# Splitting the operands of the block attention's output projection into high and low parts

## The chip, the cores and the metric

The kernel runs on one core of one Trainium2 chip. The metric is the device time of the whole program in microseconds. All times in the rows are microseconds from the start of the profiled execution's span, unless a column says ns.

## The reference

The input is `x`, 8 images of 384 channels and 32 x 32 pixels. The reference applies three layers, each added to its input: a group norm with a deformable 3 x 3 convolution, batch norm and GELU; a block attention over tokens; and an attention whose heads are chosen by a router, followed by a layer norm. Only the second matters here. With `t` the 8 x 1024 tokens of 384 channels after the first layer, cut into blocks of 128:

```python
t = t + _L1_attn_ref(_ln_t(t), w_qkv, w_ln, w_proj)
...
qkv = xb @ w_qkv                       # xb: one block of normalised tokens, 128 x 384
q, k, v = jnp.split(qkv, 3, axis=-1)
q, k = (rms(q), rms(k))                # root mean square norm over 384, times w_ln
...
q = q * cos + _rotate(q) * sin         # 12 heads of 32 channels; k in the same way
att = softmax(where(causal, q k^T / sqrt(32), -max))
y = att @ v
y = y @ w_proj                         # the output projection, 384 x 384
```

## The kernel before

The program is one launch of five stages, one after the other: `offsets_and_table`, `deform_conv`, `batch_norm_gelu`, `block_attention` and `head_attention`. In each, every engine has an instruction stream of its own, and only semaphores order them; a `wait_ge` holds back all that stands behind it on the same engine. The engines are TensorE (PE; its weight loads PEld), VectorE (DVE), ScalarE (ACT), GpSimd (POOL) and SyncE (SP).

The change lies in `block_attention` (from L902). It works on 64 blocks of 128 tokens, which stay in SBUF as `y`. The work of a block is spread over several turns, and in turn `i` different engines work on blocks `i - 1` to `i + 3`. Turn 0 is written out, turns 1 to 60 run as a hardware loop of 30 passes with two turns each (`turns`), and turns 61 to 63 are written out again. The order in each engine's `turn` is fixed by hand.

What one block goes through, with the function that does it:

- VectorE normalises the tokens into `h` (`norm`, L1066). TensorE transposes them into the bank `b_ht` (`turn_h`, L1256). ScalarE copies that, rounded to fp32r, into `h_high` (`copy_h`, L1179), and VectorE writes the remainder `b_ht - h_high` into `h_low` (`low`, L1073).
- TensorE makes Q, K and V (`make_qkv`, L1281). Each third is nine fp32r matmuls: high times high, high times low, low times high, over three chunks of 128 channels. The weights were split once ahead of the blocks: ScalarE copies `w_high` (L1240), and VectorE subtracts `w_low` (L1162).
- ScalarE sums squares of Q and K (`squares`, L1214), VectorE forms the means (`mean_square`, L1078), and GpSimd takes the power -1/2 (`rqk`, L1035). VectorE multiplies Q and K by that and by the rotation's tables (`rotate`, L1087 and L1093), and GpSimd adds the two products (L1042).
- TensorE transposes Q and K (`turn_qk`), ScalarE copies them out (`copy_qk`), and TensorE makes the 12 heads' scores and adds the causal mask by four bf16 matmuls (`scores`, L1299 and L1303).
- VectorE takes the row maxima in two halves (`maxima`, L1102 and L1108), each followed by six exponentials with their accumulator reads on ScalarE (`exponentials`, L1205). VectorE divides by the sums (`divide`, L1118 and L1121).
- TensorE transposes the probabilities (`turn_prob`, L1311), ScalarE copies them (`copy_prob`, L1184), and TensorE multiplies them with V, into `b_ht` once more (`mix`, L1324). ScalarE copies this mixed tile to `mixed_t` (`copy_mixed`, L1179).
- TensorE applies the output projection (`project`, L1332): three fp32 products over the chunks, which the trace shows as six instructions, again into `b_ht`. VectorE adds the result to `y` (`add`, L1129) and takes the tokens' statistics (`statistics`, L1137 to L1140). SyncE stores the block.

The orders around the change, in turn `i`:

- VectorE: `maxima(i)`, `norm(i+3)`, `add(i-1)`, `divide(i)` in two halves, `mean_square(i+2)`, `low(i+3)`, `rotate(i+2)`, `statistics(i-1)`. The last instruction of `statistics` is the small L1140.
- ScalarE: `copy_mixed(i-1)`, `exponentials(i)`, `squares(i+2)`, `copy_h(i+3)`, `copy_prob(i)`, `copy_qk(i+1)`, `copy_v(i+2)`.
- TensorE: `make_qkv(i+2)`, with `project(i-1)` between its first and second third, then `turn_h(i+3)`, `turn_prob(i)`, `turn_qk(i+1)`, `mix(i)`, `scores(i+1)`.

The bank `b_ht` is written in turn by `turn_h`, `mix` and `project`; `turn_h` waits for `out_done`, which `add` raises. `w_ln` holds two rows of 384 numbers that GpSimd multiplies into the tables `rot_a` and `rot_b` ahead of the blocks; it raises `tables` behind that, and VectorE and TensorE wait for `tables` first. Much SBUF is shared in time: the probabilities lie where `w_qkv` was.

Of the kernel before, what the change touches and what calls it, by code (L numbers as in the profile page):

```python
# [8 lines left out]
ACT = mybir.ActivationFunctionType  # L9
# [5 lines left out]
P = 128  # L15
BATCH, C, SIDE = 8, 384, 32
# [885 lines left out]
def block_attention(nc, io, sem, sb, bank, ident, neg_half, y, tokens, token_stats, token_rstd, block_consts, consts,  # L902
# [11 lines left out]
    with ExitStack() as mem:  # L914
        w_qkv, w_proj, rot_a, rot_b, w_ln, causal = block_consts
        ident_lo = sb(mem, "d_ident_lo", [P], BF16)
        causal_lo = sb(mem, "d_causal_lo", [CH, P], BF16)
        h = sb(mem, "d_h", [C])
        w_high = sb(mem, "d_w_high", [CH, 3 * C], F32R)
        w_low = sb(mem, "d_w_low", [CH, 3 * C], F32R)  # L920
        h_high = sb(mem, "d_h_high", [CH, P], F32R)
        h_low = sb(mem, "d_h_low", [CH, P], F32R)
        v = [sb(mem, f"d_v{u}", [C]) for u in range(2)]
        square = sb(mem, "d_square", [2, C])
        ssq = sb(mem, "d_ssq", [2])
        ms = sb(mem, "d_ms", [2])
# [10 lines left out]
                        for i in range(2))  # L937
        psum = sb(mem, "d_psum", [HEADS])
        inv = sb(mem, "d_inv", [HEADS])
        mixed_t = sb(mem, "d_mixed_t", [CH, P])  # L940
        tst = sb(mem, "d_tst", [6])
        tmv = sb(mem, "d_tmv", [1, 2])
        tvar = sb(mem, "d_tvar", [BLOCKS])
# [27 lines left out]
        pt_psum = sem("d_pt_psum")  # L971
        pt_ready = sem("d_pt_ready")
        av_psum = sem("d_av_psum")
        mt_ready = sem("d_mt_ready")
        out_psum = sem("d_out_psum")
        out_done = sem("d_out_done")
        stored = sem("d_stored")
# [16 lines left out]
        def exists(n):  # L994

            return not known(n) or 0 <= n < BLOCKS
# [13 lines left out]
        with nc.Block() as block:  # L1010
# [47 lines left out]
            def _(dve):  # L1058
# [11 lines left out]
                def low(n):  # L1070
# [2 lines left out]
                    nc.vector.tensor_tensor(h_low[:], b_ht[:, 0:C].rearrange("p (o q) -> p o q", q=P), h_high[:],  # L1073
                                            ALU.subtract).then_inc(ht_ready, 1)

                def mean_square(n):
                    dve.wait_ge(squared, n + 1)
                    nc.vector.tensor_scalar(ms[:], ssq[:], 1.0 / C, 1e-6, ALU.mult, ALU.add).then_inc(ms_ready, 1)  # L1078
# [61 lines left out]
                    nc.vector.tensor_scalar(tvar[:, blk], tmv[:, 0, 1:2], 1e-5, None, ALU.add).then_inc(token_var, 1)  # L1140

                def turn(i, u):
                    maxima(i)
                    if exists(i + 3):
                        norm(i + 3)
                    if exists(i - 1):
                        add(i - 1)
                    for half in range(2):
                        divide(i, half)
                    if exists(i + 2):  # L1150
                        mean_square(i + 2)
                    if exists(i + 3):
                        low(i + 3)
                    if exists(i + 2):
                        rotate(i + 2)
                    if exists(i - 1):
                        statistics(i - 1)
# [11 lines left out]
                low(2)  # L1169
                mean_square(1)  # L1170
                rotate(1)
                turns(turn)(dve)
                add(END)
                statistics(END)

            @block.scalar
            def _(act):
                def three(out, src):
                    return nc.scalar.activation(out, src[:, 0:C].rearrange("p (o q) -> p o q", q=P), ACT.Copy)  # L1179
# [15 lines left out]

                def copy_mixed(n):
                    act.wait_ge(av_psum, n + 1)
                    three(mixed_t[:], b_ht).then_inc(mt_ready, 1)

                def exponentials(n):  # L1200
                    for half, heads in enumerate(HALVES):
# [36 lines left out]
                act.wait_ge(consts, 16 * CONSTS)  # L1238
                for o in range(CH):
                    nc.scalar.activation(w_high[:, o], w_qkv[:, o], ACT.Copy).then_inc(w_split, 1)  # L1240
                for n in range(2):
                    copy_h(n)
                    squares(n)
                    copy_v(n, n)
# [6 lines left out]
            def _(pe):  # L1251
# [76 lines left out]

                def project(n):
                    pe.wait_ge(mt_ready, n + 1)  # L1330
                    for o in range(CH):
                        last = nc.tensor.matmul(b_ht[:, 0:C], mixed_t[:, o], w_proj[:, o], start=(o == 0),  # L1332
                                                stop=(o == CH - 1))
                    last.then_inc(out_psum, 1)

                def turn(i, u):
# [18 lines left out]
                turn_h(2)  # L1355
                turn_qk(0)
                scores(0)
                turns(turn)(pe)
                project(END)


# [1102 lines left out]
```

## Time and profile before

| | |
|---|---|
| median of 3 runs | 3693.16 us (3691.4 to 3697.67) |
| profiled execution | 3696.41 us |
| its span, first to last instruction | 3694.4 us |
| mean granted TensorE clock | 0.953 |
| TensorE busy (matmul) | 3335.8 us, 90% |
| VectorE busy | 2714.7 us, 73% |
| ScalarE busy | 2257.3 us, 61% |
| GpSimd busy | 1456.9 us, 39% |

The durations further on come from the one profiled execution. A timeline row gives the start, the duration (of all the instructions merged into the row, where x is over 1), the engine, the line, the operation, what it writes and reads with their sizes, how many instructions the row stands for, and in brackets the idle time of the engine ahead of it with the one that ended it. Successive instructions of an engine overlap in part, so the distance between two starts is less than the duration shown. Busy shares over the whole span mix stages with different limits; the block attention's loop lies between about 1705 and 2412 us.

### The profile page before, as it was taken

What the parts mean: (1) busy time and instruction counts of PE and PEld (TensorE: products, weight loads), DVE (VectorE), ACT (ScalarE), POOL (GpSimd) and SP (SyncE); (2) the same over time, 40 slices, a digit from 0 to 9 for tenths busy, and PEclk for the clock granted to TensorE, in tenths of its full rate; (3) what the DMA queues carried; (4) which work ended last, traced back from release to release, by engine and by line L of the source; (5) the groups of instructions that cost most, each with busy time, mean ns of one, the idle gap of its engine ahead of it and who ended that gap; (6) DMA issues with size and microseconds to landing.
All of it is one profiled execution on the core that took longest, in us unless ns stands there. A gap on an engine that the chain in (4) does not pass through costs nothing. (4 is left out here: it accounts for less than half of the span.)

```text
span 3694.4 us, 65555 instructions
## 1 busy us (share of the span) xinstructions
PE 3335.8 (90%) x18046; PEld 1927.0 (52%) x18046; DVE 2714.7 (73%) x5169; ACT 2257.3 (61%) x5369; POOL 1456.9 (39%) x1544
## 2 busy tenths in 40 slices
PE   7969999999999999947999999968888888888897
PEld 3434444444444444436888888844444444434443
DVE  4468888888888888756888888846677677766765
ACT  3434444444444444355777777746877778777785
POOL 2144444444444444272222222221254454544535
PEclk9979999999999999968999999978999999999997
DMA  9999989889999899541000000011222322232221
GB/s 362 370 356 345 333 333 351 324 328 338 349 340 342 336 343 347 221 171 37 17 17 17 17 17 17 17 64 45 84 74 64 91 72 65 78 87 64 59 66 55
DMA packets 230577, 647.44 MB, mean 175 GB/s; under 512 B 31142, under 2 KB 127942, under 8 KB 229958
## 3 DMA queue, kind: packets, MB, share of 16 engines
q0 software_dynamic: 82944, 453.02, 32.7%
q1 hardware_dynamic: 147398, 191.91, 16.4%
q8 instruction: 71, 1.16, 0.1%
q14 instruction: 164, 1.34, 0.1%
HBM read 520.21 MB, written 79.18 MB: 162 GB/s over the span
## 5 line engine op out<-in xcount | busy, mean ns | idle before, releaser
L697 PE MATMUL b_acc<-b_sampled,b_w 128*128 128x512 f32 x2592 | 1210.8, 594 | 0.0
L632 DVE SCALAR_TENSOR_TENSOR b_mix<-shared,b_weight,b_mix 128x384 f32<-128x384 f32 x864 | 531.8, 621 | 140.6 <-ACT b_mix L655 82.6
L697 PEld LDWEIGHTS b_acc<-b_sampled,b_w 128*128 128x128 f32 x2592 | 449.1, 191 | 347.5 <-issue 347.5
L664 ACT ACTIVATE b_sampled<-b_tps 128x384 f32<-128x384 f32 x576 | 282.7, 491 | 566.5 <-PE b_tps L715 556.6
L1988 DVE TENSOR_REDUCE e_neg_top<-e_next 128x1 f32<-128x1024 f32 x384 | 469.8, 1224 | 211.1 <-PE e_next L2301 171.4
L632 DVE SCALAR_TENSOR_TENSOR b_mix<-b_got,b_weight,b_mix 128x384 f32<-128x384 f32 x864 | 530.8, 619 | 92.6 <-ACT b_mix L655 55.9
L2140 ACT ACTIVATE e_unused<-e_next,e_neg_top 128x1024 bf16<-128x1024 f32 x384 | 430.1, 1120 | 117.1 <-DVE e_neg_top L1988 104.8
L2155 ACT ACTIVATE e_prob<-e_s 128x512 f32<-128x512 f32 x768 | 416.9, 598 | 125.3 <-PE e_s L2313 124.3
L588 POOL DMA_INDIRECT shared<-corner_table,b_index x288 | 294.7, 1023 | 418.7 <-DVE b_mix L632 291.9
L588 POOL DMA_INDIRECT b_got<-corner_table,b_index x288 | 292.6, 1016 | 356.8 <-DVE b_mix L632 282.7
L715 PEld LDWEIGHTS b_tps<-ident,b_mix 128*128 128x128 f32 x1728 | 223.0, 142 | 371.9 <-issue 328.2
L1205 ACT ACTIVATE d_w_qkv<-d_back,d_neg_top 128x128 f32<-128x128 f32 x768 | 269.6, 390 | 135.6 <-DVE d_neg_top L1108 135.6
L715 PE MATMUL b_tps<-ident,b_mix 128*128 128x128 f32 x1728 | 286.9, 275 | 57.2 <-DVE b_mix L632 50.9
L2301 PE MATMUL e_next<-e_stack 96*128 96x512 f32 x768 | 302.3, 476 | 22.6 <-issue 9.4
L2313 PE MATMUL e_s<-e_stack 98*128 98x512 f32 x768 | 271.3, 429 | 5.8 <-ACT e_prob L2155 4.8
L655 ACT ACTIVATE b_mix<-shared,b_weight 128x384 f32<-128x384 f32 x288 | 177.3, 615 | 106.5 <-ACT b_sampled L664 54.4
L2327 PE MATMUL e_acc<-e_prob,e_v 128*32 128x512 f32 x1536 | 213.4, 629 | 7.1 <-DVE e_ctx L2002 5.6
L2301 PEld LDWEIGHTS e_next<-e_stack 96*128 96x128 f32 x768 | 127.5, 198 | 159.3 <-issue 105.5
L655 ACT ACTIVATE b_mix<-b_got,b_weight 128x384 f32<-128x384 f32 x288 | 177.2, 615 | 54.5 <-ACT b_sampled L664 50.5
L1035 POOL TENSOR_TENSOR d_rqk<-d_ms,neg_half 128x2 f32<-128x2 f32 x64 | 44.9, 702 | 412.5 <-DVE d_ms L1078 412.5
L2313 PEld LDWEIGHTS e_s<-e_stack 98*128 98x128 f32 x768 | 148.8, 198 | 65.0 <-ACT e_prob L2155 34.2
L1205 ACT ACTIVATION_READ_ACCUMULATOR d_w_qkv<-d_back,d_neg_top 128x1 f32 x768 | 176.4, 230 | 0.0
(225 smaller groups left out, 5360.2 us busy)
## 6 DMA issues: line engine op xcount, KB each, us to landing
corner_table<-y SPq DMA_DIRECT2D x32, 1536.0 KB, 14.8
e_stack<-e_high SPq DMA_DIRECT2D x384, 64.0 KB, 2.0
shared<-in_x SPq DMA_DIRECT2D x8, 1536.0 KB, 10.1
c_x<-in_x SPq DMA_DIRECT2D x16, 768.0 KB, 4.4
tokens<-y SPq DMA_DIRECT2D x64, 192.0 KB, 1.9
e_tok<-tokens SPq DMA_DIRECT2D x8, 1536.0 KB, 7.3
e_stack<-e_low SPq DMA_DIRECT2D x192, 64.0 KB, 2.0
shared<-tokens SPq DMA_DIRECT2D x8, 1536.0 KB, 7.2
```

The costliest lines, as they stand in the source:

```text
L588: nc.gpsimd.indirect_dma_start(out=got[t % SLOTS][:], out_offset=None, in_=table[:, :], in_offset=bass.IndirectOffsetOnAxis(ap=index[g][:, ...
L632: ins = nc.vector.scalar_tensor_tensor(dst[:], src[:, q * C:(q + 1) * C], weight[g][:, q, k, i:i + 1], dst[:], ALU.mult, ALU.add)
L655: nc.scalar.activation(mix[t % MIXES][:], got[t % SLOTS][:, 0:C], ACT.Copy, scale=weight[g][:, 0, k, i:i + 1]).then_inc(begun, 1)
L664: nc.scalar.activation(sampled[s % 2][:, :, i * P:(i + 1) * P], tps[t % 2][:, 0:C].rearrange("p (o q) -> p o q", q=P), ACT.Copy).then_inc( ...
L697: last = nc.tensor.matmul(acc[g][co][:], w_conv[:, k, ci, co * P:(co + 1) * P], sampled[s % 2][:, ci], start=(k == 0 and ci == 0), stop=(k ...
L715: last = nc.tensor.transpose(tps[t % 2][:, o * P:(o + 1) * P], mix[t % MIXES][:, o * P:(o + 1) * P], ident[:])
L1205: last = nc.scalar.activation(prob[:, head], b_s[r][:, c * P:(c + 1) * P], ACT.Exp, bias=neg_top[:, head:head + 1], scale=SCALE, accum_out ...
L1988: nc.vector.reduce_max(neg_top[s % 2][:, t:t + 1], b_next[t % 2][:], AX.X, negate=True).then_inc(top_ready, 1)
L2140: nc.scalar.activation(unused[t % 2][:], b_next[t % 2][:], ACT.Exp, bias=neg_top[s % 2][:, t:t + 1], accum_out=den[s % 2][:, t:t + 1]).the ...
L2155: nc.scalar.activation(prob[(2 * c + f) % 8][:], b_s[f][:], ACT.Exp).then_inc(prob_ready, 1)
L2301: last = nc.tensor.matmul(b_next[t % 2][:, f * HALF:(f + 1) * HALF], stack[k][0:96, 0, t * P:(t + 1) * P], stack[k][0:96, 1, f * HALF:(f + ...
L2313: nc.tensor.matmul(b_s[f][:], stack[k][0:98, 1, c * P:(c + 1) * P], stack[k][0:98, 0, f * HALF:(f + 1) * HALF], start=True, stop=True).the ...
```

## The change

The projection's operands are split as those of `make_qkv` are. `mixed_t` goes; ScalarE writes the rounded copy `m_high`, and VectorE's new `mixed_low` writes the remainder `m_low` at the head of the turn, ahead of `maxima`. `project` waits for `m_low` and issues nine fp32r matmuls. The weights `w_proj` are split once: ScalarE's `p_high` behind the copies of `w_high`, VectorE's `p_low` behind `rotate(1)` and ahead of the turns, and TensorE waits for both ahead of the turns. To make room in SBUF, `h` and the second `v` buffer lie in the two rows of `w_ln`.

```diff
--- before.py
+++ after.py
@@ -915,12 +915,12 @@
         w_qkv, w_proj, rot_a, rot_b, w_ln, causal = block_consts
         ident_lo = sb(mem, "d_ident_lo", [P], BF16)
         causal_lo = sb(mem, "d_causal_lo", [CH, P], BF16)
-        h = sb(mem, "d_h", [C])
+        h = w_ln[:, 0]
         w_high = sb(mem, "d_w_high", [CH, 3 * C], F32R)
         w_low = sb(mem, "d_w_low", [CH, 3 * C], F32R)
         h_high = sb(mem, "d_h_high", [CH, P], F32R)
         h_low = sb(mem, "d_h_low", [CH, P], F32R)
-        v = [sb(mem, f"d_v{u}", [C]) for u in range(2)]
+        v = [sb(mem, "d_v0", [C]), w_ln[:, 1]]
         square = sb(mem, "d_square", [2, C])
         ssq = sb(mem, "d_ssq", [2])
         ms = sb(mem, "d_ms", [2])
@@ -937,7 +937,10 @@
                         for i in range(2))
         psum = sb(mem, "d_psum", [HEADS])
         inv = sb(mem, "d_inv", [HEADS])
-        mixed_t = sb(mem, "d_mixed_t", [CH, P])
+        p_high = sb(mem, "d_p_high", [CH, C], F32R)
+        p_low = sb(mem, "d_p_low", [CH, C], F32R)
+        m_high = sb(mem, "d_m_high", [CH, P], F32R)
+        m_low = sb(mem, "d_m_low", [CH, P], F32R)
         tst = sb(mem, "d_tst", [6])
         tmv = sb(mem, "d_tmv", [1, 2])
         tvar = sb(mem, "d_tvar", [BLOCKS])
@@ -971,7 +974,9 @@
         pt_psum = sem("d_pt_psum")
         pt_ready = sem("d_pt_ready")
         av_psum = sem("d_av_psum")
+        mt_high = sem("d_mt_high")
         mt_ready = sem("d_mt_ready")
+        p_split = sem("d_p_split")
         out_psum = sem("d_out_psum")
         out_done = sem("d_out_done")
         stored = sem("d_stored")
@@ -1072,6 +1077,12 @@
                     dve.wait_ge(ht_high, n + 1)
                     nc.vector.tensor_tensor(h_low[:], b_ht[:, 0:C].rearrange("p (o q) -> p o q", q=P), h_high[:],
                                             ALU.subtract).then_inc(ht_ready, 1)
+
+                def mixed_low(n):
+
+                    dve.wait_ge(mt_high, n + 1)
+                    nc.vector.tensor_tensor(m_low[:], b_ht[:, 0:C].rearrange("p (o q) -> p o q", q=P), m_high[:],
+                                            ALU.subtract).then_inc(mt_ready, 1)
 
                 def mean_square(n):
                     dve.wait_ge(squared, n + 1)
@@ -1140,6 +1151,8 @@
                     nc.vector.tensor_scalar(tvar[:, blk], tmv[:, 0, 1:2], 1e-5, None, ALU.add).then_inc(token_var, 1)
 
                 def turn(i, u):
+                    if exists(i - 1):
+                        mixed_low(i - 1)
                     maxima(i)
                     if exists(i + 3):
                         norm(i + 3)
@@ -1169,7 +1182,10 @@
                 low(2)
                 mean_square(1)
                 rotate(1)
+                dve.wait_ge(p_split, 1)
+                nc.vector.tensor_tensor(p_low[:], w_proj[:], p_high[:], ALU.subtract).then_inc(p_split, 1)
                 turns(turn)(dve)
+                mixed_low(END)
                 add(END)
                 statistics(END)
 
@@ -1195,7 +1211,7 @@
 
                 def copy_mixed(n):
                     act.wait_ge(av_psum, n + 1)
-                    three(mixed_t[:], b_ht).then_inc(mt_ready, 1)
+                    three(m_high[:], b_ht).then_inc(mt_high, 1)
 
                 def exponentials(n):
                     for half, heads in enumerate(HALVES):
@@ -1238,6 +1254,7 @@
                 act.wait_ge(consts, 16 * CONSTS)
                 for o in range(CH):
                     nc.scalar.activation(w_high[:, o], w_qkv[:, o], ACT.Copy).then_inc(w_split, 1)
+                nc.scalar.activation(p_high[:], w_proj[:], ACT.Copy).then_inc(p_split, 1)
                 for n in range(2):
                     copy_h(n)
                     squares(n)
@@ -1328,9 +1345,10 @@
 
                 def project(n):
                     pe.wait_ge(mt_ready, n + 1)
-                    for o in range(CH):
-                        last = nc.tensor.matmul(b_ht[:, 0:C], mixed_t[:, o], w_proj[:, o], start=(o == 0),
-                                                stop=(o == CH - 1))
+                    for i, (a, b) in enumerate(((m_high, p_high), (m_high, p_low), (m_low, p_high))):
+                        for o in range(CH):
+                            last = nc.tensor.matmul(b_ht[:, 0:C], a[:, o], b[:, o], start=(i == 0 and o == 0),
+                                                    stop=(i == 2 and o == CH - 1))
                     last.then_inc(out_psum, 1)
 
                 def turn(i, u):
@@ -1355,6 +1373,7 @@
                 turn_h(2)
                 turn_qk(0)
                 scores(0)
+                pe.wait_ge(p_split, 2)
                 turns(turn)(pe)
                 project(END)
```

## Rows read from the trace of the kernel before

**Rows 1.** Windows of the trace; the block loop's 60 turns; columns: engine busy us, PEclk, DMA, GB/s

```profile
1716.19:2411.22 695.03, 695.03 (x6362) 589.69 (x6361) 571.98 (x1440) 535.13 (x2160) 195.38 (x240) 1.00 0.05 17
```

**Rows 2.** Waits within the loop; columns: total us, times, longest us

```profile
ACT d_w_qkv L1205 <- DVE d_neg_top L1108: 126.3, 60, 2.2
...
DVE d_h_low L1073 <- ACT d_h_high L1179: 27.3, 60, 0.6
...
DVE d_top L1102 <- PE d_back L1303: 11.1, 30, 0.9
```

**Rows 3.** Timeline of VectorE over two turns; columns: start us, us, engine, line

```profile
1994.52 1.02 DVE L1102 TENSOR_REDUCE d_top<-d_back 128x3 f32<-128x384 f32 x2 [0.35 <-PE d_back L1303]
...
2002.30 0.62 DVE L1087 SCALAR_TENSOR_TENSOR d_part_a<-d_front,d_rqk,d_rot_a 128x384 f32<-128x384 f32 x1
...
2005.76 0.14 DVE L1140 TENSOR_SCALAR d_tvar<-d_tmv 128x1 f32 x1
...
2005.82 1.01 DVE L1102 TENSOR_REDUCE d_top<-d_back 128x3 f32<-128x384 f32 x2
...
2013.28 0.56 DVE L1073 TENSOR_TENSOR d_h_low<-d_front,d_h_high 128x384 fp32r<-128x384 f32 x1 [0.61 <-ACT d_h_high L1179]
...
2013.75 0.61 DVE L1087 SCALAR_TENSOR_TENSOR d_part_a<-d_front,d_rqk,d_rot_a 128x384 f32<-128x384 f32 x1
...
2017.20 0.14 DVE L1140 TENSOR_SCALAR d_tvar<-d_tmv 128x1 f32 x1
...
2017.69 0.56 DVE L1102 TENSOR_REDUCE d_top<-d_back 128x3 f32<-128x384 f32 x1 [0.35 <-PE d_back L1303]
```

**Rows 4.** The same two turns on ScalarE and GpSimd

```profile
1995.78 0.37 ACT L1205 ACTIVATE d_w_qkv<-d_back,d_neg_top 128x128 f32<-128x128 f32 x1 [2.24 <-DVE d_neg_top L1108]
...
1999.82 0.27 ACT L1205 ACTIVATION_READ_ACCUMULATOR d_w_qkv<-d_back,d_neg_top 128x1 f32 x1
...
2001.46 0.70 POOL L1035 TENSOR_TENSOR d_rqk<-d_ms,neg_half 128x2 f32<-128x2 f32 x1 [6.54 <-DVE d_ms L1078]
...
2004.60 0.49 ACT L1179 ACTIVATE d_mixed_t<-d_front 128x384 f32<-128x384 f32 x1
...
2011.10 0.26 ACT L1205 ACTIVATION_READ_ACCUMULATOR d_w_qkv<-d_back,d_neg_top 128x1 f32 x1
```

**Rows 5.** Last score matmuls on TensorE, and the maxima of turn 1

```profile
1715.33 0.82 PE L1303 MATMUL d_back<-d_causal_lo,d_ident_lo 128*128 128x384 bf16 x4
...
1716.19 1.02 DVE L1102 TENSOR_REDUCE d_top<-d_back 128x3 f32<-128x384 f32 x2 [0.86 <-PE d_back L1303]
...
2004.90 0.82 PE L1303 MATMUL d_back<-d_causal_lo,d_ident_lo 128*128 128x384 bf16 x4
...
2016.49 0.82 PE L1303 MATMUL d_back<-d_causal_lo,d_ident_lo 128*128 128x384 bf16 x4
```

**Rows 6.** Timeline of TensorE's weight loads (PEld) around one output projection

```profile
1994.86 0.53 PEld L1281 LDWEIGHTS d_front<-d_w_high,d_h_low 128*128 128x128 f32 x3
...
1995.38 1.65 PEld L1332 LDWEIGHTS d_front<-d_w_proj,d_mixed_t 128*128 128x128 f32 x6
...
1997.17 0.69 PEld L1281 LDWEIGHTS d_front<-d_w_high,d_h_high 128*128 128x128 f32 x3
...
1997.83 0.55 PEld L1281 LDWEIGHTS d_front<-d_w_low,d_h_high 128*128 128x128 f32 x3
```

**Rows 7.** One group by line (busy, mean ns), then timeline of prologue and tail

```profile
L1073 DVE TENSOR_TENSOR d_h_low<-d_front,d_h_high 128x384 fp32r<-128x384 f32 x60 | 33.5, 558 | 27.3 <-ACT d_h_high L1179 27.3
...
1673.50 3.27 ACT L1240 ACTIVATE d_w_high<-d_w_qkv 128x1152 fp32r<-128x1152 f32 x3 [5.92 <-PEq L774]
...
1676.84 3.89 DVE L1162 TENSOR_TENSOR d_w_low<-d_w_qkv,d_w_high 128x1152 fp32r<-128x1152 f32 x3
...
1682.13 0.97 PEld L1281 LDWEIGHTS d_front<-d_w_low,d_h_high 128*128 128x128 f32 x3
...
2445.93 3.97 PE L1332 MATMUL d_front<-d_w_proj,d_mixed_t 128*128 128x384 f32 x6 [0.61 <-ACT d_mixed_t L1179]
```

## The prediction

> **What bounds the kernel now.** I read the windows of the trace first, then the waits inside the block loop, then the timeline of single turns engine by engine. The change touches only the block attention. From the row maxima of turn 1 to those of turn 61, 60 turns, the trace spans 695.03 us, so a turn takes 11.58 us. There TensorE shows as busy all the time at granted clock 1.00, which is the 2.4 GHz level, while VectorE is busy 572 us, 9.5 us of each turn [rows 1]. Read alone, that says that TensorE is the bound and that any VectorE work fits into 2 us of idle time. The waits say to look closer. ScalarE waits for VectorE's `d_neg_top` in each of the 60 turns, 126.3 us together, over 2 us each. VectorE waits for the high half of h in 60 turns (27.3 us) and for the scores in only 30 [rows 2].
>
> So I followed VectorE and ScalarE once round, over two turns, since the loop holds two turns per pass [rows 3, 4]. Maxima start at 1994.52. ScalarE begins its exponentials 1.26 us later and issues the last accumulator read at 1999.82. Then come VectorE's second `divide`, `mean_square`, GpSimd's power (2001.46 to 2002.16) and the rotation at 2002.30, which is 2.48 us after that last read and 0.14 us after the power ends. The rotation and the statistics follow without a stall up to the last small instruction at 2005.76, and the next maxima start at 2005.82. The legs of this turn are 7.78, 3.46 and 0.06 us. The next turn's are 7.93, 3.45 and 0.49: rotation at 2013.75, last small instruction at 2017.20, maxima at 2017.69. The sum is 23.17 us, twice the 11.58 us turn. The ring is therefore nearly closed by VectorE, ScalarE and GpSimd alone. The only slack that I find is in the second turn: the rotation starts 2.65 us after the last read at 2011.10, where 2.48 would do, because the high half of h comes late from TensorE. That is 0.17 us in two turns.
>
> The trace names the scores as what ended the idle 0.35 us ahead of the maxima at 2017.69. I don't believe it. In turn 1, where VectorE had nothing else to do, the maxima began 0.86 us after the last score matmuls started (1715.33 to 1716.19); by that the scores of the pair were there at 2005.76 and 2017.35 [rows 5]. The maxima at 2017.69 were thus 0.34 us later than TensorE required. The late ones come every second turn, at the loop's edge, so I read the gap as VectorE's sequencer going round the loop.
>
> **The change, part by part.**
>
> *TensorE's projection* (`project`) loses six plain fp32 instructions and gets nine fp32r ones. Going by weight loads, the six occupy 1995.38 to 1997.17, 1.79 us, and the group behind takes 0.66 instead of 0.52 us, 0.14 more: 1.93 us. Three of the new form take 0.52 us (1994.86 to 1995.38), so nine take 1.56 us [rows 6]. TensorE saves 0.37 us a turn.
>
> *The subtraction `mixed_low`* is added on VectorE at the head of every turn, ahead of `maxima`. The nearest row is `low`: same tiles, shapes and types, 558 ns [rows 7]. Behind `low` the next instruction starts after 0.47 us (2013.28 to 2013.75) [rows 3], and that is what a queued instruction costs on the ring. It stands between the last small instruction and the maxima, exactly where VectorE has no cover in either turn. Bounds: from below, part of it hides in the loop's edge (first rival); from above, the full 0.56 us [rows 7] plus the 0.06 that the step from the last small instruction to the maxima takes [rows 3], 0.62. I take 0.47, since a wait already satisfied and registers worked out ahead cost nothing between `low` and the rotation. Its wait for `mt_high` queues `maxima`, hence ScalarE's exponentials, behind it. The wait should be empty: the copy of the mixed tile ends at 2005.09, 0.67 us ahead of the last small instruction [rows 3, 4], and TensorE, on which it depends, will be early rather than late.
>
> *The ring's new length.* 23.17 less the slack 0.17 plus 2 x 0.47 is 23.94 us in two turns, 0.77 more, or 11.97 a turn. TensorE would need only 11.58 - 0.37 = 11.21, so its saving turns into a wait of some 0.8 us ahead of `turn_prob`, where it must wait for the normalised probabilities. Thirty pairs cost +23.1 us. TensorE's term then has no weight: were the nine matmuls free, or as long as the six, the ring would stay.
>
> *`project` now waits for `m_low`* instead of the copied tile. Behind that wait stand the K and V parts of the next QKV product. TensorE reaches `project` 0.86 us after the maxima start (1994.52 and 1995.38) [rows 3, 6]; `m_low` will end 0.56 us after the point where they start now. If TensorE comes up to 0.5 us sooner, it waits at most some 0.2 us, and of its 0.8 us of new slack that costs nothing.
>
> *Splitting the projection's weights.* ScalarE's extra copy is 1,152 wide, like each of the three that take 3.27 us from 1673.50. It ends near 1677.9 and is hidden by VectorE's three subtractions, 3.89 us from 1676.84 [rows 7]. VectorE's own extra one, 3.89 / 3 = 1.3 us, stands right ahead of turn 0's maxima, which today start with no idle behind the rotation: +1.3. If `copy_h` of block 0 slipped instead, it would have until the third subtraction is done.
>
> *Edges.* Turn 1's subtraction fits in VectorE's 0.86 us of idle [rows 5]. Turn 62's costs about 0.4. In turn 63 VectorE waits long for TensorE, and it is hidden. The last block's projection is bare: six instructions take 3.97 us at the lower clock level; nine take 9 x 0.32 = 2.9 (three take 0.97 in the prologue at that level) plus some 0.2 of tail, and 0.6 goes to the subtraction [rows 7]: -0.3. Together -0.3 + 0.4 + 1.3 = +1.4.
>
> *The rest* costs nothing: h and the second v lie in `w_ln`, which GpSimd has read before `tables` lets anyone write there; the copy on ScalarE only changes its output type.
>
> **Sum:** +23.1 + 1.4 = +24.5 us. The profiled execution took 3696.4 us (span 3694.4), which gives 3721; it lies 3.3 above the median of the runs, and against the median 3693.2 the forecast is 3717.7 us, 0.7% slower.
>
> **A rule against the trace.** The gap at the loop's edge is 0.49 us where the other turn has 0.06 [rows 3], and by turn 1's 0.86 us the scores did not cause it. The Trainium skill, page "Advanced Engine Details and Errata", section "Control Flow Timing", gives a compare-and-branch about 108 ns. By that, 0.3 us of the gap would be something else, and a queued instruction could run inside it. The rows' reading stands in my sum; the rule's outcome is the first rival.
>
> **Rivals.**
> *1. The edge hides part of the subtraction.* If only about 0.1 of the 0.43 us that the edge adds is the sequencer's, 0.3 us of one subtraction in two is covered: 0.77 - 0.3 = 0.47 a pair, 14 us in thirty, 3709 with the edges. For it: the trace itself names TensorE there. Against: the 0.86 us of turn 1. Chance 0.16.
> *2. TensorE is the bound, and the kernel gets faster.* This is the plain reading of [rows 1]: 695 of 695 us busy, VectorE idle 2 us a turn. The subtraction then fits, and a turn shrinks by 0.37: 60 x 0.37 = 22 us less, plus 1.3 for the weights' split, 3672 us. It decides if the ring with the subtraction in it is shorter than 11.21 us, that is, if it has 0.77 us of slack a turn that I didn't see. Against it stands that its legs add up to the measured turn. Chance 0.10.
> *3. Gain and loss cancel.* The subtraction's 0.47 is mostly covered and TensorE's 0.37 reaches the end only in part, so the time stays within some microseconds of 3693. It needs two covers at once. Chance 0.05.
> *4. A dearer subtraction* (0.62 a turn, or a late `mt_high`): 1.07 a pair, 32 us, 3727. It lies inside the forecast's own range. Chance 0.12. That TensorE's new waits drop its clock has 0.02; the loop has no row to price it by.
> The forecast itself has 0.55.
>
> **How the numbers follow.** The time is the forecast's, 3718. The range runs from 3704, which takes in the first rival, to 3728, the dearer subtraction; outside stay the faster case, the cancelling one and the clock, 0.17. A measurement of this kernel can tell about 0.2%, 7 us, from no change. Faster has 0.10, same 0.06 (the cancelling case and the low edge of rival 1), slower 0.84.
>
> **What would show it.** Right: 60 turns take about 718 us; VectorE goes from the last small instruction through `mixed_low` to the maxima with under 0.1 us of stall in the even turns; the high half of h no longer waits for TensorE; a new wait of TensorE for the `divide` product appears, 0.5 to 1 us a turn; nine projection matmuls take 1.56 us. Wrong: turns under 11.5 us, or the maxima still ended by the scores. If the loop's edge shows less than 0.4 us between the last small instruction and `mixed_low`, rival 1 holds.

## The result and the profile after

The changed kernel takes 3719.49 us, the median of 4 runs (3718.12 to 3722.48); the kernel before, on the same chips, 3694.94 us, the median of 4 (3691.40 to 3697.67). The ratio is 1.0071, with a 95% interval of 1.0058 to 1.0083. The forecast was 3718.

The first view again is the windows of the trace, here from the maxima of turn 1 to those of turn 61. Columns as in [rows 1].

```profile
1711.47:2425.72 714.25, 682.05 (x6546) 613.88 (x6545) 597.23 (x1501) 527.19 (x2160) 195.46 (x241) 1.00 0.05 17
```

The 60 turns take 714.25 us where they took 695.03. TensorE, which showed as busy in all of the time, is now idle for 32 us of it, and the granted clock is still 1.00. The waits within this stretch, of VectorE, ScalarE and TensorE's weight loads, answer to [rows 2]:

```profile
ACT d_w_qkv L1221 <- DVE d_neg_top L1119: 169.6, 60, 3.0
...
DVE d_inv L1129 <- ACT d_w_qkv L1221: 50.9, 75, 0.9
...
DVE d_part_a L1098 <- POOL d_rqk L1040: 14.4, 59, 0.3
...
DVE d_m_low L1084 <- issue: 10.1, 29, 0.4
...
DVE d_h_low L1078 <- ACT d_h_high L1195: 0.3, 1, 0.3
...
PEld d_back L1328 <- DVE d_w_qkv L1132: 46.2, 59, 1.0
```

ScalarE's wait for `d_neg_top` has grown from 126.3 to 169.6 us. VectorE waits for the high half of h once instead of 60 times; it waits for GpSimd's power (`d_rqk`) and, mostly ahead of the second divide, for the exponentials. TensorE has a new wait in 59 of 60 turns, 46.2 us in all, 0.77 us a turn: it stands in front of `turn_prob` until VectorE has divided. Two turns of VectorE answer to [rows 3]:

```profile
1996.84 0.56 DVE L1084 TENSOR_TENSOR d_m_low<-d_front,d_m_high 128x384 fp32r<-128x384 f32 x1 [0.35 <-issue]
...
1997.32 1.01 DVE L1113 TENSOR_REDUCE d_top<-d_back 128x3 f32<-128x384 f32 x2
...
2002.89 0.19 DVE L1129 RECIPROCAL d_inv<-d_psum 128x6 f32<-128x6 f32 x1 [0.77 <-ACT d_w_qkv L1221]
...
2005.07 0.62 DVE L1098 SCALAR_TENSOR_TENSOR d_part_a<-d_front,d_rqk,d_rot_a 128x384 f32<-128x384 f32 x1 [0.30 <-POOL d_rqk L1040]
...
2008.53 0.14 DVE L1151 TENSOR_SCALAR d_tvar<-d_tmv 128x1 f32 x1
...
2008.60 0.54 DVE L1084 TENSOR_TENSOR d_m_low<-d_front,d_m_high 128x384 fp32r<-128x384 f32 x1
...
2009.06 1.01 DVE L1113 TENSOR_REDUCE d_top<-d_back 128x3 f32<-128x384 f32 x2
...
2016.71 0.62 DVE L1098 SCALAR_TENSOR_TENSOR d_part_a<-d_front,d_rqk,d_rot_a 128x384 f32<-128x384 f32 x1 [0.20 <-POOL d_rqk L1040]
...
2020.17 0.14 DVE L1151 TENSOR_SCALAR d_tvar<-d_tmv 128x1 f32 x1
...
2020.66 0.56 DVE L1084 TENSOR_TENSOR d_m_low<-d_front,d_m_high 128x384 fp32r<-128x384 f32 x1 [0.35 <-issue]
...
2021.13 1.01 DVE L1113 TENSOR_REDUCE d_top<-d_back 128x3 f32<-128x384 f32 x2
```

And on ScalarE and GpSimd, in the second of them (answering to [rows 4]):

```profile
2014.34 0.26 ACT L1221 ACTIVATION_READ_ACCUMULATOR d_w_qkv<-d_back,d_neg_top 128x1 f32 x1
...
2015.97 0.70 POOL L1040 TENSOR_TENSOR d_rqk<-d_ms,neg_half 128x2 f32<-128x2 f32 x1 [6.55 <-DVE d_ms L1089]
```

Each turn now has the subtraction L1084 between the last small instruction and the maxima. It costs 2009.06 - 2008.60 = 0.46 us in the one turn. At the loop's edge the gap of 0.49 us is there as before, with the subtraction and its 0.47 us behind it (2020.17, 2020.66, 2021.13). The pair, from 1997.32 to 2021.13, takes 23.81 us where it took 23.17. Note that the profile calls the gap at the edge "issue" now; ahead of it stand no scores that it could name. TensorE's weight loads answer to [rows 6]:

```profile
2009.48 0.54 PEld L1350 LDWEIGHTS d_front<-d_p_high,d_m_high 128*128 128x128 f32 x3
...
2010.01 0.54 PEld L1350 LDWEIGHTS d_front<-d_p_low,d_m_high 128*128 128x128 f32 x3
...
2010.53 0.54 PEld L1350 LDWEIGHTS d_front<-d_p_high,d_m_low 128*128 128x128 f32 x3
...
2011.05 0.54 PEld L1298 LDWEIGHTS d_front<-d_w_high,d_h_high 128*128 128x128 f32 x3
...
2015.87 0.20 PEld L1328 LDWEIGHTS d_back<-ident,d_w_qkv 128*128 128x128 f32 x2 [0.62 <-DVE d_w_qkv L1132]
```

The nine projection matmuls take from 2009.48 to 2011.05, 1.57 us, and the group behind them is not stretched. So TensorE did save its 0.37 us, and more than gave it back 5 us later in the wait at 2015.87.

To say where the rest of the time went, I cut every profile at five points: the first normalisation of block 0, the maxima of turn 1, the maxima of turn 61, the last block's add, and the end. The table has all the profiles of this study, one execution each, in us; the runs named there come in the next section.

```
                   ahead of    to maxima   60 turns   to the     behind
                   block 0     of turn 1              last add   it
before             1676.45     39.74       695.03     38.73      1244.45
same_before        1676.39     40.15       695.04     38.82      1244.50
padded_code        1679.13     39.43       694.54     38.97      1245.13
two_semaphores     1673.19     38.92       694.54     40.03      1241.72
after              1669.98     41.49       714.25     38.79      1253.99
same_after         1676.18     41.14       714.38     38.78      1253.82
after_padded       1675.95     41.62       714.43     39.42      1248.28
no_subtraction     1679.92     40.87       687.26     37.79      1249.06
two_subtractions   1676.77     41.95       743.05     40.97      1256.16
fp32_projection    1675.64     40.69       714.60     41.10      1251.57
four_turns         1676.16     41.06       706.76     39.13      1242.29
moved              1674.43     40.88       686.47     36.33      1247.09
moved_four         1673.82     40.56       680.83     36.21      1243.28
moved_fp32         1674.75     41.24       706.93     36.60      1248.98
```

The loop's column repeats itself to 0.2 us in the same kernel, and to 0.5 us in the two that differ from the kernel before only by idle instructions or unused semaphores. That makes it the measure for every question about the turns. The stages around the block attention do not repeat so well: 24.1 us more span in the changed kernel's first profile are +1.75, +19.22 and +0.06 in the block attention, together +21.0, and -6.5 ahead of it and +9.5 behind it. The second profiles of the two kernels differ by 29.4 us: +1.0, +19.3 and 0.0 in the block attention, together +20.3, and -0.2 ahead of it and +9.3 behind it.

### The profile page after: what moved, and what is told of

Read it like the earlier page. It is cut to its first block and busy times, and to the rows that moved or that the text cites. A ratio compares the mean times of both kernels' runs of the same rounds, so it can differ in the third digit from the quotient of the medians.

```text
span 3718.5 us, 66035 instructions
## 1 busy us (share of the span) xinstructions
PE 3329.7 (90%) x18238; PEld 1955.1 (53%) x18238; DVE 2741.6 (74%) x5234; ACT 2248.8 (60%) x5370; POOL 1454.5 (39%) x1544
## 5 line engine op out<-in xcount | busy, mean ns | idle before, releaser
L2346 PE MATMUL e_acc<-e_prob,e_v 128*32 128x512 f32 x1536 | 222.0, 652 | 7.1 <-DVE e_ctx L2021 5.5
```

The lines of the kernel that those rows point to most:

```text
L2346: last = nc.tensor.matmul(b_acc[at:at + HD], v[u][:, c, s], prob[(2 * c + f) % 8][:], start=(pair == 0), stop=(pair == PAIRS - 1))
```

## The experiments

The theory under test: a turn's length is a ring over VectorE, ScalarE and GpSimd, and what stands at the head of VectorE's turn is paid in full, while TensorE has slack. The main rival: TensorE is the bound, as its busy share says. Each experiment starts from the changed kernel, except where its text names another one. `moved` changes three places at once. The cuts in the code are marked by dots.

**The subtraction taken out (no_subtraction).**

```diff
                 def project(n):
-                    pe.wait_ge(mt_ready, n + 1)
-                    for i, (a, b) in enumerate(((m_high, p_high), (m_high, p_low), (m_low, p_high))):
+                    pe.wait_ge(mt_high, n + 1)
+                    for i, (a, b) in enumerate(((m_high, p_high), (m_high, p_low), (m_high, p_high))):
...
                 def turn(i, u):
-                    if exists(i - 1):
-                        mixed_low(i - 1)
                     maxima(i)
```

> The changed kernel without VectorE's subtraction: project waits for ScalarE's rounded copy and multiplies it a second time with p_high in the place of m_low, so the low part of the mixed tile is left out of the result. Still nine matmuls, and the weights are still split. Theory (a ring of VectorE, ScalarE and GpSimd sets the turn, TensorE has slack): the loop's pair of turns goes to the ring without the subtraction, 23.17 - 0.27 = 22.9 us, 11.45 a turn, 687 us for 60 turns, and the time to about 3694.9 - 8 + 1.3 = 3688 us. Rival (TensorE was the bound before): a turn takes 11.21 us, 673 us for 60 turns, time about 3674 us.

Measured: 60 turns in 687.26 us, pairs of 22.91; 3693.95 us in all, ratio 1.0001 (0.9992 to 1.0010). The loop says theory, within 0.3 us; TensorE's bound would have been 673. VectorE's and TensorE's waits in the loop, and one of its edges on TensorE and VectorE:

```profile
DVE d_top L1113 <- issue: 10.1, 29, 0.4
...
PEld d_back L1325 <- DVE d_w_qkv L1132: 19.8, 58, 0.5
...
2017.28 0.82 PE L1317 MATMUL d_back<-d_causal_lo,d_ident_lo 128*128 128x384 bf16 x4
...
2018.29 0.14 DVE L1151 TENSOR_SCALAR d_tvar<-d_tmv 128x1 f32 x1
...
2018.78 1.02 DVE L1113 TENSOR_REDUCE d_top<-d_back 128x3 f32<-128x384 f32 x2 [0.35 <-issue]
```

With nothing of the change left on VectorE's turns and TensorE relieved of 0.37 us a turn, the loop is only 7.8 us shorter than before, 0.13 us a turn, and TensorE waits 19.8 us for the divides. This is the most that the faster projection could bring in the old order. It also says what bound the kernel before: TensorE, which had no idle time there [rows 1], was the longer of two chains, but by only 0.13 us a turn, and past that the ring takes over. The wait rows also bear on how I read the gap ahead of the maxima. Here the last score matmuls start 1.50 us ahead of the maxima (2017.28 to 2018.78), against 1.20 before [rows 5, 3], and the gap of 0.49 us (2018.29 to 2018.78) is still there, in 29 waits of 0.35 us with no releaser. In the profile of before the same gap was put down to the scores [rows 2]. The whole time came out 6 us above what I expected; the loop did not, so that lies in the other stages of the table.

**The subtraction made twice (two_subtractions).**

```diff
                     dve.wait_ge(mt_high, n + 1)
+                    nc.vector.tensor_tensor(spare[:], b_ht[:, 0:C].rearrange("p (o q) -> p o q", q=P), m_high[:],
+                                            ALU.subtract)
                     nc.vector.tensor_tensor(m_low[:], b_ht[:, 0:C].rearrange("p (o q) -> p o q", q=P), m_high[:],
                                             ALU.subtract).then_inc(mt_ready, 1)
```

> The changed kernel with the same subtraction made twice, the first result into a part of w_proj that nobody reads any more. Theory: every microsecond at the head of VectorE's turn is paid in full, so 60 turns cost 60 x 0.47 = 28 us more than the changed kernel's 714 in the loop: 742 us, and 3748 us in all. Rival (part of what stands there hides in the loop's edge): 0.3 us less in each of 30 pairs, 3739 us. Rival (VectorE has idle time for it): no change, 3719 us.

Measured: 60 turns in 743.05 us, 28.8 us or 0.48 a turn more than the changed kernel; 3754.90 us in all, ratio 1.0155 (1.0140 to 1.0171). VectorE at the head of a turn:

```profile
2002.56 0.14 DVE L1154 TENSOR_SCALAR d_tvar<-d_tmv 128x1 f32 x1
...
2002.62 0.54 DVE L1085 TENSOR_TENSOR d_w_proj<-d_front,d_m_high 128x384 f32<-128x384 f32 x1
...
2003.09 0.54 DVE L1087 TENSOR_TENSOR d_m_low<-d_front,d_m_high 128x384 fp32r<-128x384 f32 x1
...
2003.55 1.01 DVE L1116 TENSOR_REDUCE d_top<-d_back 128x3 f32<-128x384 f32 x2
```

The rows step by 0.47 and 0.46 us. With no, one and two subtractions the loop takes 687.3, 714.3 and 743.1: 0.45 us for the first and 0.48 for the second. The first is hardly cheaper than the second, so there is no slack left in which it could have hidden. Both rivals, one with idle time and one with a cover at the edge, fall. The whole time is 7 us above the expected 3748, the loop only 1.

**The old projection behind the new wait (fp32_projection).**

```diff
-        m_high = sb(mem, "d_m_high", [CH, P], F32R)
+        m_high = sb(mem, "d_m_high", [CH, P])
...
-                    for i, (a, b) in enumerate(((m_high, p_high), (m_high, p_low), (m_low, p_high))):
-                        for o in range(CH):
-                            last = nc.tensor.matmul(b_ht[:, 0:C], a[:, o], b[:, o], start=(i == 0 and o == 0),
-                                                    stop=(i == 2 and o == CH - 1))
+                    for o in range(CH):
+                        last = nc.tensor.matmul(b_ht[:, 0:C], m_high[:, o], w_proj[:, o], start=(o == 0),
+                                                stop=(o == CH - 1))
```

> The changed kernel with the old projection behind the new wait: ScalarE copies the mixed tile unrounded, VectorE still subtracts and TensorE still waits for that, but then it issues the six plain fp32 instructions on the unrounded copy and w_proj. Theory: TensorE's 0.37 us more a turn find slack, the loop stays at 714 us and the time at 3719 us within 2 us. Rival (TensorE's saving counts in the changed kernel): 60 x 0.37 = 22 us more, 3741 us.

Measured: 60 turns in 714.60 us, against 714.25 to 714.43 in three profiles of the changed kernel's order; 3721.28 us in all, 2 above the expected 3719, ratio 1.0076 (1.0062 to 1.0090). The wait of TensorE for the divides:

```profile
PEld d_back L1328 <- DVE d_w_qkv L1132: 23.5, 58, 0.6
```

This row is the neatest of the study. TensorE works 0.37 us longer in each turn, and its wait falls from 46.2 to 23.5 us, by 22.7 us, 0.38 a turn. The loop doesn't move (at most 0.4 us in 714). In the changed kernel the nine matmuls bring nothing.

**The subtraction off the ring (moved).**

```diff
                 def turn(i, u):
-                    if exists(i - 1):
-                        mixed_low(i - 1)
                     maxima(i)
+                    if exists(i - 1):
+                        mixed_low(i - 1)
                     if exists(i + 3):
                         norm(i + 3)
+                    divide(i, 0)
                     if exists(i - 1):
                         add(i - 1)
-                    for half in range(2):
-                        divide(i, half)
+                    divide(i, 1)
...
-                        if w == 1 and between is not None:
+                        if w == 2 and between is not None:
                             project(between)
```

> The changed kernel with the subtraction taken off the ring: VectorE makes it behind maxima instead of ahead, TensorE's project stands between the second and the last third of the QKV product instead of between the first two, and VectorE's add stands between the two divides. There VectorE waits for ScalarE's exponentials anyway, 0.77 us in the changed kernel. Theory: the ring has the length that it has without the subtraction, 22.92 us a pair as measured, TensorE needs 11.21 a turn, so the loop goes from 714 to about 688 us and the time to 3694 us or a little under. Rival (the add, now late, or the projection holds the second divide): a turn stays above 11.6 us, the loop above 696 us, 3701 us or more.

Measured: 60 turns in 686.47 us; 3689.10 us in all, ratio 0.9990 (0.9981 to 0.9999) to the kernel before. The same instructions as in the changed kernel, in another order, give 27.8 us back in the loop. The loop was expected at about 688 us and the whole time at 3694 or a little under. VectorE in one turn:

```profile
2012.95 1.02 DVE L1113 TENSOR_REDUCE d_top<-d_back 128x3 f32<-128x384 f32 x2 [0.35 <-PE d_back L1320]
...
2015.21 0.55 DVE L1084 TENSOR_TENSOR d_m_low<-d_front,d_m_high 128x384 fp32r<-128x384 f32 x1
...
2016.67 0.96 DVE L1132 TENSOR_TENSOR d_w_qkv<-d_w_qkv,d_inv 128x768 f32<-128x768 f32 x1
...
2017.79 0.55 DVE L1140 TENSOR_TENSOR y<-y,d_front 128x384 f32 x1 [0.16 <-PE d_front L1350]
...
2018.54 0.19 DVE L1129 RECIPROCAL d_inv<-d_psum 128x6 f32<-128x6 f32 x1 [0.19 <-ACT d_w_qkv L1221]
```

The subtraction at 2015.21 runs while ScalarE makes the exponentials, and the second divide's reciprocal at 2018.54 comes 5.59 us behind the maxima. In the changed kernel's turn behind an edge it came 5.57 us behind them (1997.32 to 2002.89). Nothing that the ring needs has moved. How much of the gain belongs to each of the three moves, and what the moved order alone would do to the kernel before, no run here shows; but the loop is as short as with no subtraction at all (687.26 us), so the subtraction costs nothing in its new place.

**Four turns in a pass (four_turns, moved_four).**

```diff
-                with eng.Fori(0, (BLOCKS - 4) // 2) as j:
-                    turn(2 * j + 1, 1)
-                    turn(2 * j + 2, 0)
+                with eng.Fori(0, (BLOCKS - 4) // 4) as j:
+                    for k in range(1, 5):
+                        turn(4 * j + k, k % 2)
```

> The changed kernel with four turns in a pass of the loop on every engine instead of two: 15 passes. Theory (the edge costs VectorE's sequencer 0.42 us on the ring): 15 edges less give 15 x 0.42 = 6.3 us, the loop goes from 714.3 to 708 us, 3713 us in all. Rival (only about 0.1 us of the gap is the edge's): 1.6 us less. Rival (the longer loop body no longer fits where instructions are kept and each pass waits for them): a gap of more than 0.5 us at each edge, and the loop no shorter than 714 us.

Measured on the changed kernel: 60 turns in 706.76 us, 7.5 us less for 15 edges, 0.50 us an edge where 0.42 was expected; 3704.88 us in all, 8 below the expected 3713, ratio 1.0031 (1.0021 to 1.0041). The gap at VectorE's edge is there half as often as in the waits of the changed kernel (29 times, 10.1 us):

```profile
DVE d_m_low L1084 <- issue: 4.8, 14, 0.4
```

On average over the turns the gap alone is worth 0.41 us. The other 0.1 us is in the turn that follows an edge. There the rotation starts 2.47 us behind the last accumulator read, and 2.38 us behind it in the three others of a pass. In the changed kernel every second turn has the 2.47, here only every fourth.

> The moved kernel (subtraction behind maxima, projection one third later, add between the divides) with four turns in a pass of the loop. Theory: 15 edges less on the ring, each worth 0.31 us (a turn with an edge took 11.60 in the moved kernel, one without 11.29) to 0.5 us (714.3 - 706.8 in 15, measured on the changed kernel): the loop goes from 686.5 to 679 to 682 us, the time to about 3684 us. Rival (TensorE's chain through the wait for m_low, 11.22 us a turn, takes over at once): loop not under 684 us.

Measured with the moved subtraction: 60 turns in 680.83 us; 3683.08 us in all, ratio 0.9970 (0.9958 to 0.9982). This version, which leaves nothing of the computation out and has the split projection, takes 0.3% less than the kernel before and is the fastest of the study. Part of that is the fewer edges, 5.6 us for 15 of them (0.38 each in this order), which the kernel before might gain as well; that wasn't run. A turn is at 11.35 us, close to the 11.2 that TensorE needs. The whole time came within a microsecond of what was expected, the loop inside its bounds.

**The old projection in the moved order (moved_fp32).** The edit is that of fp32_projection, on the moved kernel.

> The moved kernel with the six plain fp32 instructions in the projection, on an unrounded copy and w_proj; the subtraction and the wait for it stay. Here TensorE has only 0.2 us of slack a turn: from maxima to the projection 2.86 us, from there to the next maxima 8.36 us, 11.22 together. Theory: 0.37 us more make this chain 11.59 us, longer than the ring's 11.44, so the loop goes from 686.5 to 695 to 700 us, about 3699 us in all. That would show that the nine matmuls are worth their gain only once the subtraction is off the ring. Rival (TensorE still has slack): loop 686 to 688 us.

Measured: 60 turns in 706.93 us, 20.5 more than the moved kernel, 0.34 a turn; 3712.08 us in all, ratio 1.0042 (1.0027 to 1.0058). The direction is the theory's, the size is not: I expected 9 to 14 us. The whole time is 13 us above the expected 3699. The wait of VectorE's add says why:

```profile
DVE y L1140 <- PE d_front L1349: 31.1, 58, 0.5
...
2010.59 1.01 DVE L1113 TENSOR_REDUCE d_top<-d_back 128x3 f32<-128x384 f32 x2
...
2015.80 0.56 DVE L1140 TENSOR_TENSOR y<-y,d_front 128x384 f32 x1 [0.54 <-PE d_front L1349]
2016.50 0.19 DVE L1129 RECIPROCAL d_inv<-d_psum 128x6 f32<-128x6 f32 x1
```

It waits in 58 turns, 0.54 us each (0.18 in the moved kernel), and behind it stands the second divide, which in this order comes after the add. The divide's reciprocal now starts 5.91 us behind the maxima (2010.59 to 2016.50), where it was 5.59, and waits for no exponential. So a longer projection goes straight into the ring by way of the add, and not only into TensorE's own chain of 11.59 us that I had worked out: a turn takes 11.78. In the moved order TensorE's 0.37 us count nearly in full; in the changed kernel's they count nothing.

**What drifts, and what the stage behind it does (same_before, same_after, padded_code, two_semaphores, after_padded).** The first two are the two kernels, run again. The others add only instructions that do nothing, or semaphores. The edit of padded_code, on the kernel before:

```diff
                 add(END)
                 statistics(END)
+                for _ in range(8):
+                    dve.nop(nofuse=True)
...
                 copy_mixed(END)
+                act.nop(nofuse=True)
...
                 project(END)
+                for _ in range(12):
+                    pe.nop(nofuse=True)
```

That of two_semaphores, on the kernel before:

```diff
+        unused = [sem(f"d_unused{i}") for i in range(2)]
         mt_ready = sem("d_mt_ready")
```

That of after_padded, on the changed kernel, on VectorE and in the same way on TensorE:

```diff
+                for _ in range(32):
+                    dve.nop(nofuse=True)
                 dve.wait_ge(tables, 3 + CH)
```

> The kernel before once more, for how far the other stages drift from one execution to the next. The changed kernel's profile has 6.5 us less ahead of the first block and 9.5 us more behind the last add than the profile of before. If that is drift, this profile shows differences of several microseconds in the same places, with the loop at 695 us again. If it is the change's doing (other addresses of the code or of the tiles), both stages come out within 1 us of the first profile: first normalisation at 1676, 1244 us behind the last add.

> The kernel before with instructions that do nothing behind the last turn of the block attention: 12 on TensorE, 8 on VectorE, 1 on ScalarE, about as many as the change adds to each engine's program ahead of the last stage. All four changed kernels have 4.6 to 11.7 us more behind the last add than the two profiles of before (1244.5 us). If the place of the last stage's code is the cause, this one has more than 1248 us there; if not, 1245 to 1246 us. The block loop stays at 695.0 us either way.

> The kernel before with two more semaphores that nobody uses, as many as the change adds, so that those of the last stage get the numbers that they have in the changed kernel. If the numbers matter, there are over 1248 us behind the last add; if not, 1244.5 us as before. The block loop stays at 695.0 us.

> The changed kernel once more. Its first profile had 1254.0 us behind the last add, where four profiles of before and its padded copies have 1241.7 to 1245.1. If that belongs to the changed kernel, it has over 1250 us again; if it drifts from execution to execution, it can come out at 1247 us or less. The block loop stays at 714.3 us, and the first normalisation lies between 1670 and 1680 us.

> The changed kernel with 32 instructions that do nothing at the head of the block attention on TensorE and on VectorE, where both wait some 4 us or more for the tables anyway. Both profiles of the changed kernel show 1253.8 to 1254.0 us behind the last add, that with four turns in a pass 1242.3. If the place of the last stage's code decides, this one differs from 1253.9 by over 2 us; if not, it stays within 1 us of it. The block loop stays at 714.3 us, and its turns at 11.90.

Measured, from the table: behind the last add the kernel before has 1244.45 and 1244.50 us, the changed one 1253.99 and 1253.82. So these 9.5 us are not drift: each kernel repeats its own value. Nor are they the semaphores' numbers, going by one profile: two_semaphores has 1241.72, less than the kernel before and not more. Twenty-one idle instructions in the old kernel give 1245.13, no more than 0.7 over it, against the expectation if place in the program were all. Yet 64 idle instructions ahead of the blocks take the changed kernel from 1253.9 to 1248.28, with the stage itself untouched, and a longer loop body has 1242.29. What I can say is that this stage's length goes with the program ahead of it, within a band of some 14 us over the twelve programs of the table, and that the change happened to land at the long end. When the stage begins doesn't explain it: in the two profiles of the changed kernel it begins 6 us apart and lasts the same to 0.2 us. By which mechanism stays open. The stage ahead of the blocks drifts in itself: 1669.98 and 1676.18 us in two executions of the same changed kernel.

## Why the prediction was right, and where it was not

**The ring as the bound: right.** The prediction's first step was to set the busy share of TensorE aside for the closed sum of VectorE's, ScalarE's and GpSimd's legs. The three loops with 0, 1 and 2 subtractions and the unmoved loop of fp32_projection bear it out. For the kernel before, the second rival was not all wrong: TensorE did set the turn there, but it stood only 0.13 us a turn above the ring. That is the ring's slack, mis-sized below, seen from the other side.

**TensorE's projection, 0.37 us: right in size and right to have no weight.** Nine matmuls take 1.57 us for 1.56 forecast, and the wait that swallows the saving is where it was put, at 0.77 us a turn for "some 0.8". The granted clock stayed at 1.00 in spite of these waits, so the rival with the clock falls too.

**The subtraction, 0.47 us: right.** 0.46 and 0.47 us in the rows, 0.48 by the doubled one. The dearer subtraction of 0.62 us falls.

**The ring's slack: the term that was mis-sized.** The prediction put 0.17 us into a pair of turns, all of it in the turn where the high half of h came late, and held the other turn's 2.48 us from last accumulator read to rotation for a floor. In the changed kernel this leg takes 2.37 us in the turn that ends at the edge (2014.34 to 2016.71); in that turn the rotation starts 0.04 us after GpSimd's power ends (2015.97 + 0.70). The 2.48 us hold only for the turn behind an edge. In no_subtraction a pair takes 22.91 instead of 23.17, so the slack was 0.26 and not 0.17. A pair is 23.81 and not 23.94, and thirty of them make +19.2 instead of +23.1. The slack accounts for 0.09 of these 0.13 us; the other 0.04 are spread over legs that changed by some hundredths each.

**The loop's edge: right.** The first rival had some 0.3 us of it hide the subtraction. The gap stays 0.49 us with TensorE early, and taking 15 edges away gave 0.50 us each (0.38 in the moved order). The Trainium skill, "Advanced Engine Details and Errata", section "Control Flow Timing", has 108 ns for a compare-and-branch; whatever else the edge contains, it costs the changed kernel's ring over four times that. What it consists of no run shows.

**Weights and edges: right, as far as it can be told.** Forecast +1.4 us, measured +1.75 ahead of the maxima of turn 1 and +0.06 behind those of turn 61 in the first profiles, +1.0 and 0.0 in the second. Two executions of the same kernel differ by 0.4 us ahead of turn 1, so the 0.4 between forecast and measurement says nothing. The weights' subtraction stands bare, 1.27 us from 1699.22 to the maxima at 1700.49, for 1.3 forecast:

```profile
1699.22 1.35 DVE L1186 TENSOR_TENSOR d_p_low<-d_w_proj,d_p_high 128x1152 fp32r<-128x1152 f32 x1
...
1700.49 1.02 DVE L1113 TENSOR_REDUCE d_top<-d_back 128x3 f32<-128x384 f32 x2
```

The last block's projection runs with TensorE at its lower level, 1.2 GHz (granted clock 0.54 from 2461.31 to 2464.50), so that three weight loads take 0.97 us here and 0.54 in the loop; the nine matmuls save more there than in a turn, and that pays for the subtraction. From the subtraction at 2460.70 to the add at 2464.51 it takes 3.81 us, against 4.02 us before, from the first of the six instructions to the add at 2449.95 [rows 7]: 0.2 us less, where 0.3 was forecast.

```profile
2460.70 0.56 DVE L1084 TENSOR_TENSOR d_m_low<-d_front,d_m_high 128x384 fp32r<-128x384 f32 x1 [3.19 <-ACT d_m_high L1195]
...
2462.12 0.97 PEld L1350 LDWEIGHTS d_front<-d_p_low,d_m_high 128*128 128x128 f32 x3
...
2464.51 0.55 DVE L1140 TENSOR_TENSOR y<-y,d_front 128x384 f32<-128x384 f32 x1 [3.25 <-PE d_front L1350]
```

**The sum: right in part by chance.** In the first profiles the change costs 21.0 us in the block attention, where 24.5 were forecast, 3.9 too much in the loop and 0.4 too little around it. The measured difference of the medians is 24.55. The remainder of 3.5 us is in stages that the change doesn't touch and that the prediction held for constant; in the first profiles they are -6.5 and +9.5, in the second -0.2 and +9.3. The sign and the mechanism would have held without them; the agreement to 1.5 us would not.

## What to carry to other kernels

An engine that shows as busy all the time can be the bound by next to nothing, here 0.13 us in a turn of 11.58: add the legs of the other engines' chain from one instruction to the same one a turn later, and if they make up nearly the whole turn, that chain takes over at once. A short instruction added to such a chain cost its full step in every turn here, whatever the idle share of its engine, and the same instruction put where that engine waits anyway cost nothing; look for that place first, and move the consumer with it. Time a stage by its own landmarks in the trace, since the total of a long program moves by some microseconds for reasons of its own.

## What the runs showed of the hardware that I had not expected

The last stage, identical in all the kernels, takes 1241.7 to 1256.2 us behind the last add, depending on the program ahead of it, and repeats to 0.2 us in each of the two programs that ran twice. An edge of the hardware loop costs the chain through VectorE 0.50 us in the changed kernel and 0.38 in the moved order; 0.4 of it shows as a gap ahead of the first instruction, and 0.1 in the turn that follows. And the profile's name for what ended a wait was very likely wrong at this place in the kernel before: it named the scores for a gap that stayed at 0.49 us when the scores came 0.3 us earlier.
